# Two attention and feed-forward layers: the row maxima's products over all 72 rows on the whole TensorE array, and one load for each head's stack

## The chip, the core and the metric

One core of one Trainium2 chip runs the kernel as one program. The metric is the time of one execution on the device in microseconds (us). TensorE does the matrix products and writes to PSUM, VectorE and ScalarE compute and read PSUM out, GpSimd computes in SBUF, and SyncE issues most of the DMAs.

## What is computed

Two transformer layers over x of 8 x 512 x 128, each with a normalisation, attention of 16 heads of 8 dimensions and a feed-forward part (a block-quantised one in the first layer, 9 experts in the second). The change touches attention, which both layers have alike:

```python
xn = _layernorm(x, axis=-1)
# for each of 8 sequences of 512 tokens, 16 heads, d = 8
scores = jnp.einsum('bthd,bshd->bhts', q, k) / np.sqrt(HEAD_DIM)
weights = jax.nn.softmax(scores, axis=-1)
attn = jnp.einsum('bhts,bshd->bthd', weights, v).reshape(B, T, C)
x = x + attn @ w_out + b_out + ffn(xn)
```

## The kernel before, in words

**Precision by parts.** q and k are split into three bf16 parts each (`parts`, NP = 3). A score is the sum over the nine pairs of parts and over the 8 dimensions of a head, so it is one matmul over 9 x 8 = 72 rows, a "stack". Before the exponential the row's maximum must be taken off. It is computed first, from products alone, negated, split into two bf16 rows (`nm_hl`) and put under the stack of q as two more rows, against ones in the stack of k. So the scores of layer l come from `ks[l]` and `qs[l]` over 74 rows.

**Two passes over the scores.** The first pass is `maxima` (a pair of heads hp, a tile t of 128 tokens: two products of 128 x 512 into the two banks of a pair buffer `mx`; VectorE reduces both at once, L743) and `tile_maxima` (one product into a bank of the ring, one head and tile at a time, reduced at L747). It uses `products` (L1039): only 8 of the 9 pairs of parts, NQK = 8, which are HALF = 64 rows. Heads with even number keep these in partitions 0 to 63, odd ones in 64 to 127 (`main_rows`), so the two products of a pair lie in different halves of the array. The second pass is `scores` (L1091), on the whole array: 74 rows for even heads, all 128 for odd ones, whose unused rows hold zeros. Its results are exponentiated by ScalarE (L563) and weighted sums follow (`weighted_sums`, L1083).

**The order of TensorE** is written out by hand in `turn`, one turn for each of the 8 sequences (seven in a loop, then "last"). A turn has: the slots 3 to 15 of layer 0's scores and sums; the projections, with four pairs of the next sequence's layer 0 maxima; the nine experts, four chunks each, where a chunk is one product `expert_hidden` (L970), then zero or two pairs of maxima (`maxima_of_chunk`), then a quarter of the output of the expert before (`expert_out`, L1141, 8 matmul records); and the 16 slots of layer 1's scores and sums, of which slots 1 to 12 also hold two `tile_maxima` of layer 0. In a full turn 24 of the chunks have two pairs (experts 0 to 8: 1, 2, 2, 2, 4, 4, 3, 3, 3); in the last one only the 16 of layer 1 (experts 3 to 7). VectorE follows the same list and has between the reductions, once for each expert, `add_expert` (L831). There are two pair buffers and two ring banks.

**Stacks.** SyncE stores the parts to DRAM (`store_parts`, eight DMAs: six for the 8 pairs in `scratch`, two for the ninth in `rest`), waits for them, and loads them back (`load_stacks`): for each head one DMA of 64 rows for k and one for q, and behind eight or sixteen heads four DMAs with the ninth pair's 8 rows (`rest_rows`). The maxima wait for the 64 rows (`stack_in`), the scores for the rest too (`rest_in`). `max_rows_of` puts the maxima's two rows in, four DMAs, since even and odd heads have them in different partitions. `set_ones` on GpSimd fills zeros and ones once, four memsets a layer.

**Ahead of the loop** the first sequence's layer 0 goes through the same steps up to slot 2 of its scores, with all 32 pairs of its maxima.

Of the kernel before, what the change touches and what calls it, by code (L numbers as in the profile page):

```python
# [12 lines left out]
P = 128  # L13
# [3 lines left out]
NP = 3  # L17
NQK = NP * NP - 1
HALF = NQK * HD
# [31 lines left out]


def main_rows(u):

    return slice(u * HALF, u * HALF + HALF)


def rest_rows(u):

    return slice(HALF - HD, HALF) if u else slice(HALF, HALF + HD)  # L60


def max_row(u, a):

    return HALF - HD - 2 + a if u else HALF + HD + a


def score_rows(u):

    return slice(0, P) if u else slice(0, HALF + HD + 2)  # L70

# [102 lines left out]
def two_layers(nc, x, w_qkv, w_out0, b_out0, w_gate, w_up, w_down, wqT, wkT, wvT, woT, bq, bk, bv, bo,  # L174
               wr1, br1, wr2, br2, w1, b1, w2, b2, scratch, rest, out):
    ring, accs, mxs = ring_uses()
    ctx = ExitStack()
    with ctx:
# [83 lines left out]
        rest_in = [sem("rest_in0"), sem("rest_in1")]  # L262
# [9 lines left out]
        N_WEIGHT_DMAS, N_FP4_DMAS, N_STORES, N_STACK, N_ROWS = 17, 7, 16 * 8, 16 * 4, 16 * 4  # L272
# [42 lines left out]
        def _(sp):  # L315
# [40 lines left out]
            def store_parts(l, values):  # L356
# [4 lines left out]
                by_row = scratch[l].rearrange("m h (d n) t -> m (h d) n t", n=NQK)  # L361
                last_row = rest[l].rearrange("m h d t -> m (h d) t")
                for i in range(NP):
                    n = slice(NP * i, min(NP * i + NP, NQK))
                    width = n.stop - n.start
                    sp.dma_start(by_row[0, :, n, :], parts[:, i:i + 1, 0, :].broadcast_to([P, width, T])).then_inc(scratch_out, 16)
                    sp.dma_start(by_row[1, :, n, :], parts[:, 0:width, 1, :]).then_inc(scratch_out, 16)
                for m in range(2):
                    sp.dma_start(last_row[m], parts[:, NP - 1, m, :]).then_inc(scratch_out, 16)
                sp.wait_ge(scratch_out, stored)  # L370

            def load_stacks(l, first, last):

                for h in range(first, last):
                    for m, dst in ((1, ks[l]), (0, qs[l])):
                        sp.dma_start(dst[main_rows(h % 2), h, :], scratch[l, m, h]).then_inc(stack_in[l][h // 2], 16)
                for m, dst in ((1, ks[l]), (0, qs[l])):
                    for u in range(2):
                        heads = slice(first + u, last, 2)
                        sp.dma_start(dst[rest_rows(u), heads, :], rest[l, m, heads].rearrange("h d t -> d h t")).then_inc(rest_in[l], 16)  # L380
# [929 lines left out]
```

## Time and profile before

| | us |
|---|---|
| median of 3 runs | 1623.88 |
| lowest, highest | 1618.66, 1624.66 |
| the profiled execution, own time | 1616.24 |
| its span, first to last instruction | 1614.5 |

| engine | busy us | share | instructions |
|---|---|---|---|
| TensorE, matmul (PE) | 1465.2 | 91% | 8221 |
| TensorE, weight load (PEld) | 663.5 | 41% | 8253 |
| VectorE (DVE) | 1112.0 | 69% | 2019 |
| ScalarE (ACT) | 822.1 | 51% | 1007 |
| GpSimd (POOL) | 102.7 | 6% | 138 |

The mean granted clock of TensorE is 0.966 of its 2.4 GHz. Matmul records overlap, since they are pipelined: the time that a product takes of the engine is read from the start of one to the start of the next, not from a record's length. An fp32 product of 512 columns appears as two records. In the views, PEld is the load of a matmul's stationary operand.

### The profile page before, as it was taken

To read this page: it belongs to the slowest core of one execution; us is meant where nothing else is said; L and a number is where in the kernel's file an instruction comes from. 1 tells how busy PE (TensorE), PEld (TensorE's weight loads), DVE (VectorE), ACT (ScalarE), POOL (GpSimd) and SP (SyncE) were. 2 spreads that over 40 slices of the span, in tenths; PEclk is the share of its full clock that TensorE was granted. 3 is DMA by queue.
4 is the path that set the end of the run, shared out by engine and by line. 5 is a ranking of instruction groups with operands and counts; after the bars stand their busy time and mean duration, and the time that the engine had idled before them with its cause. 6 is when DMAs were issued, how large, how long until landed. Compare 5 with 4: busy or idle time off the path is not lost.

```text
span 1614.5 us, 23856 instructions
## 1 busy us (share of the span) xinstructions
PE 1465.2 (91%) x8221; PEld 663.5 (41%) x8253; DVE 1112.0 (69%) x2019; ACT 822.1 (51%) x1007; POOL 102.7 (6%) x138
## 2 busy tenths in 40 slices
PE   2689999999989999889998999999998999997997
PEld 1124552245523554245532455234542355423561
DVE  8976884778756787567956688477875678653660
ACT  1164238742576426754277423874257642684336
POOL 5001000110000100010001100001000100001000
PEclk7689999999999999999999999999999999997999
DMA  4404300241002400034000420024100240000300
GB/s 114 160 16 140 87 2 9 68 129 47 2 16 87 128 22 2 16 113 123 2 2 30 148 73 1 9 72 130 42 2 16 91 130 16 2 9 28 90 2 7
DMA packets 93994, 87.90 MB, mean 54 GB/s; under 512 B 12890, under 2 KB 93091, under 8 KB 93619
## 3 DMA queue, kind: packets, MB, share of 16 engines
q1 hardware_dynamic: 92258, 83.59, 17.1%
q0 software_dynamic: 672, 2.16, 0.5%
q8 instruction: 77, 1.26, 0.3%
q10 hardware_dynamic: 944, 0.54, 0.1%
q14 instruction: 43, 0.34, 0.1%
HBM read 45.87 MB, written 39.85 MB: 53 GB/s over the span
## 4 chain that ended last, share of the span: by engine, by line
PE 53%; DVE 21%; issue 14%; DVEq 5%; ACT 4%; POOL 2%; SPq 0%; DMA 0%; ACTq 0%; POOLq 0%
PE ring L970 15%; PE sums L1141 14%; DVE nm L743 8%; PE mx L1091 8%; PE sums L1083 7%; PE mx L1039 5%; ACT ex L563 3%; DVEq L825 2%; PE ring L976 2%; DVE macc L831 2%; PE ring L1039 2%; DVE xn L671 1%; PE ring L965 1%; POOL parts L470 1%; DVE h_sb L719 1%
## 5 line engine op out<-in xcount | busy, mean ns | idle before, releaser
L563 ACT ACTIVATE ex<-mx 128x1024 f32<-128x1024 f32 x512 | 497.2, 1027 | 162.2 <-PE mx L1091 161.7
L743 DVE TENSOR_REDUCE nm<-mx 128x2 f32<-128x1024 f32 x428 | 501.2, 1216 | 85.6 <-PE mx L1039 81.4
L605 ACT ACTIVATE ex<-ring,b_sb 128x512 f32<-128x512 f32 x288 | 197.1, 687 | 421.5 <-PE ring L970 421.4
L1141 PEld LDWEIGHTS sums<-w_sb,ex 128*128 128x128 f32 x2304 | 283.5, 191 | 94.8 <-issue 89.9
L1141 PE MATMUL sums<-w_sb,ex 128*128 128x128 f32 x2304 | 319.3, 283 | 0.4
L970 PE MATMUL ring<-xnT,w_sb 128*128 128x512 f32 x576 | 297.6, 602 | 2.0 <-ACT ex L605 2.0
L1091 PE MATMUL mx<-qs,ks 74*128 74x512 bf16 (+1 forms) x992 | 274.8, 385 | 15.7 <-ACT ex L563 6.6
L1083 PE MATMUL sums<-ex,vs 128*18 128x512 f32 x2048 | 269.0, 600 | 14.4 <-issue 13.8
L1091 PEld LDWEIGHTS mx<-qs,ks 128*128 128x128 bf16 (+1 forms) x1024 | 75.9, 98 | 261.8 <-ACT ex L563 235.4
L1039 PE MATMUL mx<-ks,qs 64*128 64x512 bf16 x856 | 149.4, 396 | 36.0 <-DVE nm L743 34.8
L747 DVE TENSOR_REDUCE nm<-ring 128x1 f32<-128x512 f32 x168 | 108.2, 686 | 72.3 <-PE ring L1039 71.9
L1039 PEld LDWEIGHTS mx<-ks,qs 64*128 64x128 bf16 x856 | 34.3, 94 | 220.2 <-issue 112.0
L831 DVE SCALAR_TENSOR_TENSOR macc<-sums,w,macc 128x128 f32<-128x128 f32 x288 | 81.1, 344 | 40.7 <-PE sums L1141 30.6
L970 PEld LDWEIGHTS ring<-xnT,w_sb 128*128 128x128 f32 x576 | 88.5, 192 | 23.7 <-ACT ex L605 8.8
L1083 PEld LDWEIGHTS sums<-ex,vs 128*18 128x18 f32 x2048 | 35.4, 96 | 107.5 <-issue 105.0
L766 DVE COPY work<-sums 128x512 f32<-128x512 f32 x32 | 22.0, 687 | 81.1 <-PE sums L1083 81.1
L475 POOL DMA_DIRECT2D out<-macc x8 | 6.4, 799 | 1012.1 <-DVE macc L783 1012.1
L470 POOL TENSOR_TENSOR parts<-qk_f,parts 128x512 bf16<-128x512 f32 x32 | 36.4, 1158 | 222.7 <-DVE parts L683 222.7
L736 DVE TENSOR_TENSOR acc<-acc,ring 128x512 f32<-128x512 f32 x8 | 5.5, 688 | 51.1 <-PE ring L1018 51.1
L965 PE MATMUL ring<-ident,xn 128*128 128x128 f32 x64 | 11.4, 304 | 28.4 <-DVE xn L671 28.4
L516 ACT COPY hqT<-ring 128x512 f32<-128x512 f32 (+1 forms) x40 | 22.7, 593 | 22.0 <-PE ring L965 22.0
L1039 PE MATMUL ring<-ks,qs 64*128 64x512 bf16 x168 | 32.8, 387 | 0.0
(135 smaller groups left out, 1017.2 us busy)
## 6 DMA issues: line engine op xcount, KB each, us to landing
scratch<-parts SPq DMA_DIRECT2D x64, 384.0 KB, 4.0
ks<-scratch SPq DMA_DIRECT2D x256, 64.0 KB, 2.2
qs<-scratch SPq DMA_DIRECT2D x256, 64.0 KB, 2.2
scratch<-parts SPq DMA_DIRECT2D x32, 256.0 KB, 4.1
w_sb<-w SPq DMA_DIRECT2D x2, 2304.0 KB
rest<-parts SPq DMA_DIRECT2D x32, 128.0 KB, 3.2
x_sb<-x SPq DMA_DIRECT2D x8, 256.0 KB, 2.8
out<-macc POOLq DMA_DIRECT2D x8, 256.0 KB, 3.8
```

What stands on the lines that cost most here:

```text
L470: last = pool.tensor_tensor(parts[:, 2, m, :], qk_f[:, m, :], parts[:, 1, m, :], ALU.subtract)
L563: act.activation(ex[:, ex_buffer(l, k), 2 * i:2 * i + 2, :], mx[bank][:, :, :], ACT.Exp, scale=SCALE).then_inc(mx_free[bank], 1)
L605: act.activation(ex[:, e % 2, c, :], bank[:, :], ACT.Silu, bias=b1_sb[:, e * EC + c:e * EC + c + 1]).then_inc(free, 1)
L743: dve.tensor_reduce(nm[l][:, t, h:h + 2], mx[bank][:, :, :], AX.X, ALU.max, negate=True).then_inc(mx_free[bank], 1)
L747: dve.tensor_reduce(nm[0][:, t, h:h + 1], bank[:, :], AX.X, ALU.max, negate=True).then_inc(free, 1)
L825: dve.drain()
L831: last = dve.scalar_tensor_tensor(macc[:, t, :], acc[bank][:, t * P:(t + 1) * P], w9[:, t, e:e + 1], macc[:, t, :], ALU.mult, ALU.add)
L970: pe.matmul(bank[0:rows, 0:width], lhsT, rhs, start=True, stop=True).then_inc(full, 1)
L1039: return pe.matmul(bank, qs[l][r, h, t * P:(t + 1) * P], ks[l][r, h, :], start=True, stop=True)
L1083: last = pe.matmul(acc[bank][32 * j:32 * j + 2 * VW, :], values[:, start:start + 2 * VW], ex[:, ex_buffer(l, k), j, :], start=q == 0 and s ...
L1091: return pe.matmul(bank, ks[l][r, h, s * P:(s + 1) * P], qs[l][r, h, :], start=True, stop=True)
L1141: last = pe.matmul(acc[bank][:, t * P:(t + 1) * P], ex[:, e % 2, c, t * P:(t + 1) * P], w2_sb[:, e, c, :], start=c == 0, stop=c == EC - 1)
```

## The change

The stack of each head has all 72 rows in partitions 0 to 71 (`SK`), and the maxima's rows are 72 and 73 for every head (`SKM` = 74). `products` runs over the 72 rows, all nine pairs of parts, and `scores` over 74 for every head. The array `rest`, its stores, loads and waits are gone: six stores, one load for each head and operand, two DMAs for the rows of maxima. The ones are set by one memset of partitions 64 to 127 of `ks` for each layer, and `qs` isn't set.

```diff
-NQK = NP * NP - 1
-HALF = NQK * HD
+SK = NP * NP * HD
+SKM = SK + 2
...
-        N_WEIGHT_DMAS, N_FP4_DMAS, N_STORES, N_STACK, N_ROWS = 17, 7, 16 * 8, 16 * 4, 16 * 4
+        N_WEIGHT_DMAS, N_FP4_DMAS, N_STORES, N_STACK, N_ROWS = 17, 7, 16 * 2 * NP, 16 * 4, 16 * 2
...
-                for m in range(2):
-                    sp.dma_start(last_row[m], parts[:, NP - 1, m, :]).then_inc(scratch_out, 16)
...
                 for h in range(first, last):
                     for m, dst in ((1, ks[l]), (0, qs[l])):
-                        sp.dma_start(dst[main_rows(h % 2), h, :], scratch[l, m, h]).then_inc(stack_in[l][h // 2], 16)
-                for m, dst in ((1, ks[l]), (0, qs[l])):
-                    for u in range(2):
-                        heads = slice(first + u, last, 2)
-                        sp.dma_start(dst[rest_rows(u), heads, :], rest[l, m, heads].rearrange("h d t -> d h t")).then_inc(rest_in[l], 16)
+                        sp.dma_start(dst[0:SK, h, :], scratch[l, m, h]).then_inc(stack_in[l][h // 2], 16)
...
                 for a in range(2):
-                    for u in range(2):
-                        r = max_row(u, a)
-                        sp.dma_start(qs[l][r:r + 1, first + u:last:2, :], nm_hl[u:last - first:2, a, :]).then_inc(done, 16)
+                    sp.dma_start(qs[l][SK + a:SK + a + 1, first:last, :], nm_hl[0:last - first, a, :]).then_inc(done, 16)
...
-            set_ones(0)
+            pool.memset(ks[0][64:P, :, :].bitcast(FP32), TWO_ONES).then_inc(ones_set, 1)
...
             def products(l, bank, h, t):
 
-                r = main_rows(h % 2)
-                return pe.matmul(bank, qs[l][r, h, t * P:(t + 1) * P], ks[l][r, h, :], start=True, stop=True)
+                return pe.matmul(bank, qs[l][0:SK, h, t * P:(t + 1) * P], ks[l][0:SK, h, :], start=True, stop=True)
...
-                r = score_rows(h % 2)
-                return pe.matmul(bank, ks[l][r, h, s * P:(s + 1) * P], qs[l][r, h, :], start=True, stop=True)
+                return pe.matmul(bank, ks[l][0:SKM, h, s * P:(s + 1) * P], qs[l][0:SKM, h, :], start=True, stop=True)
...
-                pe.wait_ge(rest_in[1], (it + 1) * N_STACK)
                 pe.wait_ge(nm_row_in[1], it * N_ROWS + N_ROWS)
```

## Rows read from the trace of the kernel before

**Rows 1.** The page's part 4: the chain that ended last, by engine, by line.
```profile
PE 53%; DVE 21%; issue 14%; DVEq 5%; ACT 4%; POOL 2%; SPq 0%; DMA 0%; ACTq 0%; POOLq 0%
PE ring L970 15%; PE sums L1141 14%; DVE nm L743 8%; PE mx L1091 8%; PE sums L1083 7%; PE mx L1039 5%; ACT ex L563 3%; DVEq L825 2%; PE ring L976 2%; DVE macc L831 2%; PE ring L1039 2%; DVE xn L671 1%; PE ring L965 1%; POOL parts L470 1%; DVE h_sb L719 1%
```

**Rows 2.** The page's part 5: groups, xcount | busy, mean ns | idle before.
```profile
L743 DVE TENSOR_REDUCE nm<-mx 128x2 f32<-128x1024 f32 x428 | 501.2, 1216 | 85.6 <-PE mx L1039 81.4
L1039 PE MATMUL mx<-ks,qs 64*128 64x512 bf16 x856 | 149.4, 396 | 36.0 <-DVE nm L743 34.8
```

**Rows 3.** Timeline of PE, experts 6 and 5: start us, us, what, idle before.
```profile
589.72 1.02 PE L970 MATMUL ring<-xnT,w_sb 128*128 128x512 f32 x2
590.58 1.05 PE L1141 MATMUL sums<-w_sb,ex 128*128 128x128 f32 x8
591.47 1.02 PE L970 MATMUL ring<-xnT,w_sb 128*128 128x512 f32 x2
592.43 0.60 PE L1039 MATMUL mx<-ks,qs 64*128 64x512 bf16 x4
592.96 1.16 PE L1141 MATMUL sums<-w_sb,ex 128*128 128x128 f32 x8
593.96 1.02 PE L970 MATMUL ring<-xnT,w_sb 128*128 128x512 f32 x2
```

**Rows 4.** Timeline of PE: maxima that wait for VectorE, in experts 5, 6, 8.
```profile
583.29 0.39 PE L1039 MATMUL mx<-ks,qs 64*128 64x512 bf16 x2 [0.74 <-DVE nm L743]
...
594.91 0.75 PE L1039 MATMUL mx<-ks,qs 64*128 64x512 bf16 x4
...
614.64 0.39 PE L1039 MATMUL mx<-ks,qs 64*128 64x512 bf16 x2 [0.19 <-DVE nm L743]
```

**Rows 5.** Timelines of PE and PEld: scores between expert outputs, and both kinds' weight loads.
```profile
620.23 1.03 PE L1091 MATMUL mx<-qs,ks 74*128 74x512 bf16 x4
621.09 1.95 PE L1141 MATMUL sums<-w_sb,ex 128*128 128x128 f32 x16
...
592.42 0.11 PEld L1039 LDWEIGHTS mx<-ks,qs 64*128 64x128 bf16 x4 [0.76 <-issue]
...
620.12 0.64 PEld L1091 LDWEIGHTS mx<-qs,ks 74*128 74x128 bf16 x4
```

**Rows 6.** Timeline of DVE, from the addition in expert 5 to the next.
```profile
579.85 1.13 DVE L831 SCALAR_TENSOR_TENSOR macc<-sums,w,macc 128x128 f32<-128x128 f32 x4 [0.17 <-issue]
580.89 4.61 DVE L743 TENSOR_REDUCE nm<-mx 128x2 f32<-128x1024 f32 x4
...
591.00 1.12 DVE L831 SCALAR_TENSOR_TENSOR macc<-sums,w,macc 128x128 f32<-128x128 f32 x4 [0.17 <-issue]
```

**Rows 7.** Timelines of PE and ACT: one slot of layer 1 with two tiles.
```profile
625.14 1.04 PE L1091 MATMUL mx<-qs,ks 74*128 74x512 bf16 x4
626.12 0.39 PE L1039 MATMUL ring<-ks,qs 64*128 64x512 bf16 x2
626.43 1.05 PE L1083 MATMUL sums<-ex,vs 128*18 128x512 f32 x8
...
625.79 1.94 ACT L563 ACTIVATE ex<-mx 128x1024 f32<-128x1024 f32 x2 [0.34 <-PE mx L1091]
```

**Rows 8.** Timeline of POOL and DVE ahead of the loop.
```profile
9.55 5.58 POOL L481 MEMSET ks<- 32x2048 f32 x3
...
30.10 1.22 DVE L702 TENSOR_SCALAR qsc<-amax 128x22 f32<-128x22 f32 x1
...
31.76 0.18 DVE L707 TENSOR_SCALAR qrs<-qrs 128x22 f32<-128x22 f32 x1
...
50.98 13.66 DVE L743 TENSOR_REDUCE nm<-mx 128x2 f32<-128x1024 f32 x12
```

**Rows 9.** Timelines of SP and PE: a stack load's issue, and the first product on it.
```profile
514.70 0.60 SPq L376 DMA_DIRECT2D qs<-scratch  x1
...
518.84 0.39 PE L1039 MATMUL mx<-ks,qs 64*128 64x512 bf16 x2
```

**Rows 10.** Windows: the stretch, busy us by engine, PEclk, DMA share, GB/s.
```profile
529.46:532.87 3.41, 3.41 (x10) 1.75 (x8) 2.37 (x3) 0.67 (x1) 0.00 (x0) 0.50 0.36 102
```

More of the change, by code:

```diff
@@ L50, in head @@
     return (g // 2 * HG + j) * 2 + g % 2
[L53 to L70, printed above, removed]
 class Ring:
@@ L174, in two_layers @@
 def two_layers(nc, x, w_qkv, w_out0, b_out0, w_gate, w_up, w_down, wqT, wkT, wvT, woT, bq, bk, bv, bo,
-               wr1, br1, wr2, br2, w1, b1, w2, b2, scratch, rest, out):
+               wr1, br1, wr2, br2, w1, b1, w2, b2, scratch, out):
     ring, accs, mxs = ring_uses()
@@ L418, in turn @@
                     load_max_rows(0, rows0)
-            sp.wait_ge(ones_set, 4)
+            sp.wait_ge(ones_set, 1)
             store_parts(0, stack_values(0, 0))
@@ L475, in store_out @@
                 pool.dma_start(out_rows[bass.ds(it * T, T), :].rearrange("(t p) c -> p t c", p=P), macc[:, :, :]).then_inc(macc_free, 16)
-            def set_ones(l):
-                for n, (rows, first, value) in enumerate([(qs[l][0:HALF], 1, 0.0), (ks[l][0:32], 1, 0.0),
-                                                          (ks[l][32:HALF], 1, TWO_ONES), (ks[l][HALF:HALF + 32], 0, TWO_ONES)]):
-                    pool.memset(rows[:, first:NH:2, :].bitcast(FP32), value).then_inc(ones_set, 1)
-                    pool.wait_ge(ones_set, l * 4 + n + 1)
             rstd_of(0, 0)
             pool.wait_ge(rstd_ready[0], 1)
-            set_ones(0)
+            pool.memset(ks[0][64:P, :, :].bitcast(FP32), TWO_ONES).then_inc(ones_set, 1)
+            pool.wait_ge(ones_set, 1)
             third_part(0, 0)
             pool.wait_ge(p3_ready, 1)
-            set_ones(1)
+            pool.memset(ks[1][64:P, :, :].bitcast(FP32), TWO_ONES).then_inc(ones_set, 1)
+            pool.wait_ge(ones_set, 2)
             pool.wait_ge(weights_in, 16 * N_WEIGHT_DMAS)
@@ L1303 @@
     args = {name: nc.dram_tensor(name, v.shape, FP32, kind="ExternalInput").ap() for name, v in arrays.items()}
-    scratch = nc.dram_tensor("scratch", (2, 2, NH, HALF, T), BF16, kind="Internal").ap()
-    rest = nc.dram_tensor("rest", (2, 2, NH, HD, T), BF16, kind="Internal").ap()
+    scratch = nc.dram_tensor("scratch", (2, 2, NH, SK, T), BF16, kind="Internal").ap()
     out = nc.dram_tensor("out", (B, T, P), FP32, kind="ExternalOutput").ap()
-    two_layers(nc, **args, scratch=scratch, rest=rest, out=out)
+    two_layers(nc, **args, scratch=scratch, out=out)
     r = run_bass_kernel_spmd(nc, [arrays], core_ids=[0])
```

15 lines of the change are left out of this document (5 added, 10 removed).

## The prediction

> **What bounds the kernel now.** I read the chain of work that ended last first: 53% of it is TensorE (PE) and 21% VectorE (DVE), and its longest lines are the two expert products, the reductions and the maxima's own matmuls [rows 1]. So I ask of each stretch whether PE or DVE sets its pace. The groups by line give the counts: 856 products into the pair buffers, that is 428 pairs, and 428 reductions of 1.22 us [rows 2]; by the code another 7 x 12 = 84 pairs go into the ring banks. A plain chunk of the experts on PE (one hidden product, one quarter of an output) takes 0.86 + 0.89 = 1.75 us: 589.72 to 590.58 to 591.47 [rows 3]. A chunk with two pairs between them takes 0.96 + 0.53 + 1.00 = 2.49 us (591.47, 592.43, 592.96, 593.96) [rows 3]. I call these four products a quad. So a quad costs 0.73 us of PE although its own rows last 0.53: the hidden product before it and the output after it are each 0.10 longer. There PE never idles, so PE sets the pace. In experts 4 and 5, where every chunk has a quad, DVE takes its share: a quad's second pair at 583.29 has PE idle for 0.74 us until a reduction ends [rows 4], and from one addition on DVE to the next (579.85 to 591.00) it is 11.15 us, against 4 x 2.49 = 9.96 of PE alone [rows 6]. In the twelve slots of layer 1 with two tiles, PE is without a pause while ScalarE waits 0.34 us for it [rows 7].
>
> **Part 1: the products go from two halves of the array to the whole array.** Lost is their concurrency. Today two products of a quad start together, and the quad lasts 0.53; four products over 74 rows, also bf16 with 512 columns, take 621.09 - 620.23 = 0.86 us, 0.215 each [rows 5]. 72 rows are nearest to these 74, so I take 0.865 for a quad and 0.43 for a pair. Gained are the edges. The weights of half-array products are loaded only at 592.42, after 0.76 us in which nothing is loaded, while the hidden product still runs; those of the 74-row products are loaded from 620.12 on, ahead of the first matmul at 620.23 and under the product before it [rows 5]. So the 0.10 at either side should go: a chunk with a quad becomes 1.755 + 0.865 = 2.62 us instead of 2.49. A quad costs 0.135 more, where PE sets the pace.
> The Trainium skill (TensorEngine Tiling (Array Packing), Key Properties) says that changing the tiling mode drains TensorE, which agrees with those 0.10 us. The same page (Theoretical Speedup) gives half-array packing up to twice the speed for 64 rows or fewer. That rule speaks against this change; taken alone it would charge each of 512 pairs 0.215 us, some 110 us.
>
> Stage by stage, for one of the seven full turns:
> - Experts 0 to 3: 7 quads, no wait now, 7 x 0.138 = 0.97 us (2.62 against 2.482 by the starts unrounded).
> - Experts 4 and 5: I step through the two pair buffers. Reductions follow each other every 1.13 us (four in 4.61) and a buffer is free again 1.27 us after its reduction starts (the second of 580.89 starts at 582.02, its buffer is written at 583.29) [rows 4, 6]. A pair's reduction can start some 0.65 us after its first product (0.215 until the second starts, 0.39 of that one, 0.04 of signal; 0.39 is a row's length [rows 3]). With the expert's first quad at 0, DVE is first held by the addition and reduces from 1.57 and 2.70; the second quad comes at 2.62, waits until 2.84, its second pair until 3.97, and it ends at 4.40; the others come at 6.16 and 8.78 without a wait, the next expert's at 11.40. The same reckoning of the kernel before gives 11.25 where the trace has 11.15 [rows 6], so it is good to 0.1. Like against like, each of the two costs 11.40 - 11.25 = 0.15, together 0.30 and not 8 x 0.138 = 1.10, because part of what they took was waiting for DVE.
> - Experts 6 and 7: 3 quads each, 3 x 0.138, less the 0.14 us by which one quad of each waits for DVE (0.75 where others last 0.60 [rows 3, 4]) and which the longer quad covers: 0.27 each, 0.53.
> - Expert 8: 3 quads, less the wait at 614.64 [rows 4], 0.58 - 0.21 = 0.37 us by the starts of the pairs: 0.04.
> - Sum of the experts: 0.97 + 0.30 + 0.53 + 0.04 = 1.84 us. The last turn has only layer 1's 16 quads, those of experts 3 to 7: 0.28 + 0.30 + 0.53 = 1.11.
> - Twelve slots: from the first score (625.14) over the pair (626.12) to the sums (626.43) it is 1.29 us today, with an edge of 0.10 before the pair and one after it [rows 7]. After, six full-array products follow each other and one edge is left: 6 x 0.215 + 0.10 = 1.39, and 0.01 that the first score takes more: 1.40. So 0.107 a slot, 12 x 0.107 = 1.28 us. ScalarE's 0.34 of waiting shows that it doesn't take over.
> - Four single pairs in layer 0's projections: 0.43 against 0.32 + 0.10, about 0.1 us together.
> A full turn: 1.84 + 1.28 + 0.10 = 3.22; seven of them 22.5; with the last turn 23.7 us.
>
> **Part 2: one load of 72 rows for a head, no loads of a rest.** Sixteen stack loads of 72 rows take the place of those of 64, at 0.60 us of issue each [rows 9], and the four rest loads behind them go, with two of eight stores. No transfer gets nearer to the end: in layer 0 the first head pair's fourth load is issued at 514.70, and the first product on it runs at 518.84 [rows 9]. Even if 72 rows took half as long again as 64, that is 0.3 us of issue for each of four loads, 1.2 us, and the load issued at 514.70 would be late by no more than the stores that went give back. Bounds: -0.5 to +0.5 us a turn; I take 0. What hides it is those 4 us between issue and use; without them a late load would cost its lateness once a turn. The PE waits for the rest are removed; none of them is what PE idles for, so 0. The loads of the rows of maxima fall from four to two at a time, which matters only ahead of the loop, below.
>
> **Part 3: the constants, ahead of the loop.** Three of the four memsets on GpSimd last 5.58 us together, and a second set follows; the new ones cover half the elements in one piece, an estimated 3.6 us instead of 7.4 each. DVE's small tensor-scalar operations are held by them: one of 22 elements at 30.10 takes 1.22 us, where its like at 31.76 takes 0.18 [rows 8]. That one is freed (-1.0), others are held as long by one long memset as by two short ones (-0.3 to +0.4). Two row loads less ahead of the first x load, at 0.60 an issue [rows 9]: up to -1.2, I take -0.9. Against it: in the first maxima DVE sets the pace (12 reductions in 13.66 us [rows 8]). Should PE have half its clock there, as in [rows 10], a pair takes 2 x 0.43 = 0.86 instead of 0.43, and a reduction is ready some 0.09 us late on every second pair: for 24 pairs 24 x 0.045 = +1.1. Together -1.1, bounds -3 to +2.
>
> **Sum.** 23.7 - 1.1 = 22.6 us on the profiled execution, 1616.24 us (span 1614.5): 1639. That execution was quicker than all three runs, 1618.66 to 1624.66. On their median, 1623.88, it is 1646.
>
> **Rivals.**
> A, the edges stay: 72-row products lie between fp32 products and pay 0.10 at each side as now. For: the slots' scores keep such an edge toward the sums [rows 7]. Against: the 74-row products between expert outputs have none [rows 5]. A quad then costs 0.33 more; with the waits that it covers 5.8 us a turn of experts, 12 x 0.215 in slots, 4 x 0.215 in projections: 9.2 x 7 + 3.5 = 68, less 1.1: 67, 1691 on the median.
> B, not slower: PE's clock. In every turn PE idles before the second norm's transposes, and then 529.46 to 532.87 runs at 0.50 of 2.4 GHz with PE busy for all 3.41 us [rows 10]; six turns show this one drop, and near the start of the loop and in the last turn there are three more, with two of them longer. One short drop costs half its length, 1.7 us; all together some 18 us. The new turn is 3.2 us longer, so the idle stretch falls elsewhere in the clock's own rhythm. If all drops vanished: 1616.2 + 22.6 - 18 = 1621, 0.3% above, on the median 1629. It decides once at least 15 of the 18 us come back. Against: the idle stretch itself stays as long as it is.
> C, the same clock the other way: the loop's first 2 us of idle start to cause a drop as well, 8 x 1.7 = +14: 1661.
> D, the stacks are late: one load's lateness a turn; at 1 us, +7: 1654.
>
> **How the numbers follow.** The forecast (PE pays 0.11 to 0.14 a quad or slot, drops about as now) has 0.72; A 0.06; B 0.10; C 0.07; D 0.05. The likeliest gives 1646. B's 1629 and C's 1661 with a little for the runs' spread make the range 1628 to 1664, which leaves out A and part of the rest. A measurement of this kernel can tell about 0.5%, 8 us, from no change. B gives the 0.08 of no change and, if the start gives back more too, 0.02 of faster; everything else is slower, 0.90.
>
> **What would show it.** Right: the maxima's matmuls at 72 rows start 0.215 apart, their weights load while the product before runs, a chunk with a quad lasts 2.62 us, the slots' period grows from 2.28 to 2.39, experts 4 and 5 take 11.3 to 11.5 us, and PE's idle for reductions shrinks. Wrong: a chunk with a quad at 2.8 (A), a table of the granted clock with fewer or more stretches at 0.50 (B, C), PE waiting for a stack load (D), or DVE running ahead of PE in experts 4 and 5, which would show that I sized their waits badly.

## The result, and the profile after

| | before | after |
|---|---|---|
| median of 4 runs each, us | 1621.99 | 1639.3 |
| lowest, highest | 1618.66, 1624.66 | 1638.69, 1639.9 |
| the profiled execution, own time | 1616.24 | 1639.9 |
| its span | 1614.5 | 1637.6 |
| its mean granted clock | 0.966 | 0.967 |

The ratio is 1.0109, with a 95% interval of 1.0085 to 1.0132: the change makes the kernel 1.1% slower. Between the medians lie 17.3 us, between the two profiled executions 23.1 us of span. That difference has a cause of its own, and the experiments come back to it.

The chain that ended last, the page's part 4 of the kernel after, by engine and by line (before: [rows 1]):

```profile
PE 59%; DVE 18%; issue 14%; ACT 4%; DVEq 3%; POOL 2%; DMA 0%; SPq 0%; ACTq 0%; POOLq 0%
PE ring L934 16%; PE sums L1103 14%; PE mx L1002 9%; PE mx L1053 8%; PE sums L1046 7%; DVE nm L707 6%; ACT ex L527 3%; PE ring L1002 2%; PE ring L940 2%; PE ring L929 1%; DVE xn L635 1%; DVEq L789 1%; POOL parts L439 1%; DVE h_sb L683 1%; DVE h_sb L673 1%
```

The lines have moved up by 36 to 38: the maxima's products are L1002 now, the hidden product L934, the expert output L1103, the reductions L707 and L711, the scores L1053. TensorE's share of the chain went from 53 to 59%, that of the maxima's products in it from 5 to 9%, and VectorE's fell from 21 to 18%. The groups say the same (busy us, mean ns, then the idle time before them and what ended it; before: [rows 2]):

```profile
L707 DVE TENSOR_REDUCE nm<-mx 128x2 f32<-128x1024 f32 x428 | 502.9, 1218 | 99.6 <-PE mx L1002 99.4
L1002 PE MATMUL mx<-ks,qs 72*128 72x512 bf16 x856 | 239.3, 394 | 22.6 <-DVE nm L707 21.0
```

A reduction costs what it cost (1218 against 1216 ns). TensorE is busy with the products for 239.3 us instead of 149.4, waits for reductions 21.0 us instead of 34.8, and VectorE waits for the products 99.4 us instead of 81.4.

The timeline of TensorE in the experts (start us, us, what, idle before), with one chunk without maxima and one with four of them, as in [rows 3], and two rows of its weight loads:

```profile
598.31 1.02 PE L934 MATMUL ring<-xnT,w_sb 128*128 128x512 f32 x2
599.17 1.05 PE L1103 MATMUL sums<-w_sb,ex 128*128 128x128 f32 x8
600.06 1.02 PE L934 MATMUL ring<-xnT,w_sb 128*128 128x512 f32 x2
600.92 1.03 PE L1002 MATMUL mx<-ks,qs 72*128 72x512 bf16 x4
601.78 1.06 PE L1103 MATMUL sums<-w_sb,ex 128*128 128x128 f32 x8
602.68 1.02 PE L934 MATMUL ring<-xnT,w_sb 128*128 128x512 f32 x2
...
600.49 0.10 PEld L1002 LDWEIGHTS mx<-ks,qs 72*128 72x128 bf16 x1 [0.24 <-issue]
600.92 0.53 PEld L1002 LDWEIGHTS mx<-ks,qs 72*128 72x128 bf16 x3 [0.33 <-issue]
```

The plain chunk takes 0.86 + 0.89 = 1.75 us, as before. The one with a quad takes 0.86 + 0.86 + 0.90 = 2.62 (600.06 to 602.68). The hidden product before a quad lasts 0.86 again and not 0.96, the output behind it 0.90 and not 1.00, and the first weights are loaded at 600.49, under the hidden product, where they used to load only as the product started [rows 5]. This is the chunk that the prediction laid out, to 0.01 us.

**Where the 23.1 us lie.** I cut both traces at the same instructions (first products of each expert, of each layer's sums) and took differences, after minus before:

| stretch | us |
|---|---|
| ahead of the loop | +1.1 |
| experts 1 to 8, seven full turns | 7 x 1.80 = +12.6 |
| experts of the last turn | +1.2 |
| slots of layer 1, seven turns | 7 x 1.11 = +7.8 |
| projections and expert 0's begin, eight turns | -8.6 |
| loop's first slots, eight turns | +6.9 |
| from a turn's last sums to the next turn, and the end | +2.1 |
| sum | +23.1 |

Of the last +2.1, 1.2 lie at the end, where TensorE's last products ran at half clock, and 0.9 in the pauses between turns. In the row of the projections stands the one quad of expert 0 too. The two large rows besides the experts and slots are not the work of the maxima: they are stretches of half clock that left one place and came up in another, as these windows of the kernel after show (stretch, then us, busy us by engine, PEclk, DMA share, GB/s; before: [rows 10]):

```profile
482.20:485.60 3.40, 3.23 (x16) 0.53 (x16) 2.78 (x14) 0.00 (x0) 1.03 (x1) 0.50 0.24 69
536.80:540.20 3.40, 3.40 (x9) 1.64 (x8) 2.47 (x3) 0.69 (x1) 0.00 (x0) 0.51 0.00 0
871.40:874.80 3.40, 3.40 (x17) 0.53 (x10) 2.87 (x15) 0.00 (x0) 1.03 (x1) 0.51 0.15 43
```

The second is the old place, in the projections ahead of the experts; one of the full turns still has it. The first and third are new: right after the pause in which TensorE waits at the loop's start. Before, six turns had a drop in the projections and none of these six had one at the loop's start; after, one has it in the projections and four at the loop's start. A drop that goes from the projections gives back 1.4 to 1.5 us, one at the loop's start takes 1.61 to 1.66.

### The profile page after: what moved, and what is told of

Read it like the earlier page. It is cut to its first block, busy times and chain, and to the rows that moved or that the text cites. A ratio compares the mean times of both kernels' runs of the same rounds, so it can differ in the third digit from the quotient of the medians.

```text
span 1637.6 us, 23699 instructions
## 1 busy us (share of the span) xinstructions
PE 1509.7 (92%) x8253; PEld 724.2 (44%) x8253; DVE 1110.4 (68%) x2019; ACT 822.0 (50%) x1007; POOL 95.0 (6%) x132
## 4 chain that ended last, share of the span: by engine, by line
PE 59%; DVE 18%; issue 14%; ACT 4%; DVEq 3%; POOL 2%; DMA 0%; SPq 0%; ACTq 0%; POOLq 0%
PE ring L934 16%; PE sums L1103 14%; PE mx L1002 9%; PE mx L1053 8%; PE sums L1046 7%; DVE nm L707 6%; ACT ex L527 3%; PE ring L1002 2%; PE ring L940 2%; PE ring L929 1%; DVE xn L635 1%; DVEq L789 1%; POOL parts L439 1%; DVE h_sb L683 1%; DVE h_sb L673 1%
## 5 line engine op out<-in xcount | busy, mean ns | idle before, releaser
L707 DVE TENSOR_REDUCE nm<-mx 128x2 f32<-128x1024 f32 x428 | 502.9, 1218 | 99.6 <-PE mx L1002 99.4
L1103 PEld LDWEIGHTS sums<-w_sb,ex 128*128 128x128 f32 x2304 | 298.3, 191 | 62.8 <-issue 34.2
L1103 PE MATMUL sums<-w_sb,ex 128*128 128x128 f32 x2304 | 301.2, 275 | 0.2
L934 PE MATMUL ring<-xnT,w_sb 128*128 128x512 f32 x576 | 296.9, 602 | 2.0 <-ACT ex L569 2.0
L1053 PE MATMUL mx<-qs,ks 74*128 74x512 bf16 x1024 | 282.6, 385 | 11.4 <-ACT ex L527 6.5
L1046 PE MATMUL sums<-ex,vs 128*18 128x512 f32 x2048 | 276.3, 615 | 15.3 <-issue 14.7
L1002 PE MATMUL mx<-ks,qs 72*128 72x512 bf16 x856 | 239.3, 394 | 22.6 <-DVE nm L707 21.0
L1053 PEld LDWEIGHTS mx<-qs,ks 74*128 74x128 bf16 x1024 | 76.5, 98 | 265.8 <-ACT ex L527 216.5
L1002 PEld LDWEIGHTS mx<-ks,qs 72*128 72x128 bf16 x856 | 73.6, 99 | 214.4 <-issue 107.0
L711 DVE TENSOR_REDUCE nm<-ring 128x1 f32<-128x512 f32 x168 | 108.3, 686 | 80.1 <-PE ring L1002 80.1
L934 PEld LDWEIGHTS ring<-xnT,w_sb 128*128 128x128 f32 x576 | 88.7, 192 | 22.1 <-ACT ex L569 8.4
L1002 PE MATMUL ring<-ks,qs 72*128 72x512 bf16 x168 | 50.1, 379 | 0.0
```

The source lines that it names most:

```text
L707: dve.tensor_reduce(nm[l][:, t, h:h + 2], mx[bank][:, :, :], AX.X, ALU.max, negate=True).then_inc(mx_free[bank], 1)
L711: dve.tensor_reduce(nm[0][:, t, h:h + 1], bank[:, :], AX.X, ALU.max, negate=True).then_inc(free, 1)
L934: pe.matmul(bank[0:rows, 0:width], lhsT, rhs, start=True, stop=True).then_inc(full, 1)
L1002: return pe.matmul(bank, qs[l][0:SK, h, t * P:(t + 1) * P], ks[l][0:SK, h, :], start=True, stop=True)
L1046: last = pe.matmul(acc[bank][32 * j:32 * j + 2 * VW, :], values[:, start:start + 2 * VW], ex[:, ex_buffer(l, k), j, :], start=q == 0 and s ...
L1053: return pe.matmul(bank, ks[l][0:SKM, h, s * P:(s + 1) * P], qs[l][0:SKM, h, :], start=True, stop=True)
```

## The experiments

Each ran beside the kernel before on the same chip; ratios are to that. "The stretch of expert 4" is from the first output product of one expert to that of the next, the first of the two with four quads.

### One half of the array for all

Do the edges of 0.10 us belong to products on a half of the array, or to the change between bf16 and fp32 products? The kernel after, with 64 of its 72 rows:

```diff
-                return pe.matmul(bank, qs[l][0:SK, h, t * P:(t + 1) * P], ks[l][0:SK, h, :], start=True, stop=True)
+                return pe.matmul(bank, qs[l][0:64, h, t * P:(t + 1) * P], ks[l][0:64, h, :], start=True, stop=True)
```

> The changed kernel with the maxima's products over rows 0 to 63 of every stack (left out: the ninth pair of parts and the last rows of the eight), so all products lie in one half of the array, one behind the other. My theory (what the change pays is lost concurrency, what it gets back is the 0.10 us edge on either side of half-array products): products 0.215 us apart as in the changed kernel, but with both edges back, so a chunk with a quad lasts 2.8 us instead of 2.62, a slot's pair 0.53 with its edge before it; the time is about 1680 us, 40 to 45 above the changed kernel, ratio to the kernel before 1.03 to 1.04. Rival (the edges belong to two halves being at work together, not to 64 rows): the same as the changed kernel, 1639, ratio 1.01. Rival (cost goes with rows): a little under 1639.

Measured: 1704.4 us (1699.38 to 1708.13), ratio 1.0498 (1.046 to 1.0535), slower than the kernel after by 65 us although it multiplies fewer rows. TensorE's timeline:

```profile
598.75 1.02 PE L934 MATMUL ring<-xnT,w_sb 128*128 128x512 f32 x2
599.71 1.03 PE L1002 MATMUL mx<-ks,qs 64*128 64x512 bf16 x4
600.67 1.16 PE L1103 MATMUL sums<-w_sb,ex 128*128 128x128 f32 x8
601.66 1.02 PE L934 MATMUL ring<-xnT,w_sb 128*128 128x512 f32 x2
...
602.62 0.60 PE L1002 MATMUL mx<-ks,qs 64*128 64x512 bf16 x2
...
602.62 0.11 PEld L1002 LDWEIGHTS mx<-ks,qs 64*128 64x128 bf16 x2 [0.76 <-DVE nm L707]
```

The hidden product takes 0.96 again (598.75 to 599.71), the output 0.99, and the weights load only at 602.62, together with the product's start and after 0.76 us of nothing, as in [rows 5]. So the edges belong to products on 64 rows, and the change from 64 to 72 rows is what removes them; the types are the same in both. A third part of the price I had not reckoned with: the quad lasts 0.96 and not 0.86. Its products still start 0.215 us apart; the 0.10 more lies behind the last of them, before the output starts. Two views cut close show it, of this run and of the kernel before:

```profile
600.15 0.59 PE L1002 MATMUL mx<-ks,qs 64*128 64x512 bf16 x2
600.67 0.38 PE L1103 MATMUL sums<-w_sb,ex 128*128 128x128 f32 x1
```

```profile
592.43 0.60 PE L1039 MATMUL mx<-ks,qs 64*128 64x512 bf16 x4
592.96 0.49 PE L1141 MATMUL sums<-w_sb,ex 128*128 128x128 f32 x2
```

Here two products from 600.15 take 0.52 until the output, not 0.43. In the kernel before, four side by side are two steps of 0.215, again 0.43, and take 0.53. So the third 0.10 was there before the change too, hidden in the quad's 0.53. A chunk costs 2.91 us against 2.62. Over a turn the experts take 5.4 us more and the slots 1.2, some 50 us of the 65 in all; the rest lies ahead of the loop, in the projections and in stretches of half clock (mean clock 0.961). My expectation of the size was too small, since I had given this third border nothing.

### Two halves on the new layout

Is anything of the rest of the change (stores, loads, memsets, rows of maxima) worth time? The kernel after, with the products side by side on two halves again. The odd heads' operand on rows 64 to 127 is a stand-in with the same shape:

```diff
-                return pe.matmul(bank, qs[l][0:SK, h, t * P:(t + 1) * P], ks[l][0:SK, h, :], start=True, stop=True)
+                r = slice(64 * (h % 2), 64 * (h % 2) + 64)
+                left = ks if h % 2 else qs
+                return pe.matmul(bank, left[l][r, h, t * P:(t + 1) * P], ks[l][r, h, :], start=True, stop=True)
```

> The changed kernel with its one-load stacks, its memsets and its two row loads kept, but a pair's two products side by side again: even heads over rows 0 to 63, odd heads over rows 64 to 127, where the data are a stand-in (left out: the odd heads' true maxima; softmax doesn't change with what is taken off). It isolates the loads, stores and memsets. My theory (they are off the path): the time of the kernel before less up to 2 us, ratio 0.998 to 1.001, chunks with a quad at 2.48 and experts 4 at 11.16 us. Rival (part of the 17 us comes from stack loads of 72 rows or from their stores): the ratio stays at 1.003 or more, with waits on DMA in the trace.

Measured: 1622.22 us (ten runs, 1616.27 to 1631.1), ratio 1.0014 (0.9988 to 1.004): no change that can be measured. At equal granted clock (the lines are drawn further below) its runs stand 0.5 us under those of the kernel before. Cut as above, all experts and slots stand within 0.01 us of the kernel before; only ahead of the loop, at the drops and in the pause between turns is there a difference. So the loads, the stores, the memsets and the 74-row scores cost and bring nothing that can be told, and all that the change costs comes with one line, the products over 72 rows.

### Half the reduction, after and before

The prediction lets the waits for VectorE hide part of a quad's price. Take VectorE out of the way in both kernels: the reductions read 256 of the 512 columns.

```diff
-                dve.tensor_reduce(nm[l][:, t, h:h + 2], mx[bank][:, :, :], AX.X, ALU.max, negate=True).then_inc(mx_free[bank], 1)
+                dve.tensor_reduce(nm[l][:, t, h:h + 2], mx[bank][:, :, 0:256], AX.X, ALU.max, negate=True).then_inc(mx_free[bank], 1)
...
-                dve.tensor_reduce(nm[0][:, t, h:h + 1], bank[:, :], AX.X, ALU.max, negate=True).then_inc(free, 1)
+                dve.tensor_reduce(nm[0][:, t, h:h + 1], bank[:, 0:256], AX.X, ALU.max, negate=True).then_inc(free, 1)
```

> The changed kernel with every reduction of maxima over the first 256 of 512 columns (left out: the other columns), so VectorE never sets the pace in the experts. To be read against e4. My theory (in experts 4 and 5 VectorE hides part of the price): a chunk with a quad lasts 2.62 everywhere, four of them 10.5 us instead of 11.42, total about 1610 to 1620. Rival (VectorE hides nothing): experts 4 and 5 stay near 11.4 and the distance to e4 equals that of the two kernels, 17 to 23 us.

> The kernel before with every reduction of maxima over the first 256 of 512 columns (left out: the other columns). My theory: a chunk with a quad lasts 2.48 everywhere, four of them 9.93 us instead of 11.16, total about 1575 to 1585, so that e3 is 30 to 38 us above it: 184 quads at 0.138 and 84 slots at 0.107 are 34 us with nothing hidden, against the 21 or so of the two kernels themselves. Rival: e3 minus e4 is 17 to 23 us.

Measured: after 1612.18 us (1603.92 to 1619.05, ratio 0.9933), before 1572.73 (1569.72 to 1574.57, ratio 0.97). Between the two lie 39.5 us of medians and 33.6 us of span in the profiled executions (1601.7 and 1568.1). The groups of the kernel before with half the reduction, then of the kernel after with it:

```profile
L743 DVE TENSOR_REDUCE nm<-mx 128x2 f32<-128x512 f32 x428 | 276.1, 685 | 231.9 <-PE mx L1039 231.5
L1039 PE MATMUL mx<-ks,qs 64*128 64x512 bf16 x856 | 138.7, 393 | 7.9 <-DVE nm L743 7.5
```

```profile
L707 DVE TENSOR_REDUCE nm<-mx 128x2 f32<-128x512 f32 x428 | 277.4, 686 | 258.9 <-PE mx L1002 258.0
L1002 PE MATMUL mx<-ks,qs 72*128 72x512 bf16 x856 | 232.3, 391 | 4.7 <-DVE nm L707 4.2
```

With a reduction of 685 ns TensorE waits 7.5 and 4.2 us in all, and the stretch of expert 4 is plain TensorE work: four chunks in 9.95 us (4 x 2.49) before, in 10.47 (4 x 2.62) after. The change now costs the experts 3.0 us a turn instead of 1.8. In the two experts with four quads, from one addition on VectorE to the next, it is 0.53 each (9.95 to 10.48), where with whole reductions it is 0.26 each (11.16 to 11.42). That is the price without cover. The medians are no clean measure of it: at a granted clock of 0.971, which runs of both had, the distance is 31 us and not 39.5. The other way round: cheaper reductions are worth 49 us to the kernel before and 27 to the one after by the medians (part of the 49 is clock, 0.971 against 0.963), and in experts and slots 3.8 and 2.4 us a turn. TensorE's side by side products are what lets a faster VectorE pay.

### Other places for the maxima, before and after

If VectorE sets the pace in experts 4 and 5 and TensorE in experts 1 to 3, the list of pairs can be evened. Both kernels with layer 1's pairs spread:

```diff
-M1_BY_EXPERT = [0, 0, 0, 4, 8, 8, 6, 6, 0]
+M1_BY_EXPERT = [0, 0, 0, 8, 6, 6, 6, 6, 0]
```

> The kernel before with layer 1's maxima spread as 8, 6, 6, 6, 6 pairs over experts 3 to 7 instead of 4, 8, 8, 6, 6; nothing left out. My theory: PE waits for reductions only behind an expert with eight pairs, some 1.3 us each time; one such expert in place of two saves 1.2 us in each of eight turns: 1610 to 1614, ratio 0.993 to 0.995. Rival (the waits go with the number of pairs, wherever they are): no change, 1.000.

> The changed kernel with the same spread, 8, 6, 6, 6, 6. My theory: four chunks with quads in a row cost it 11.42 us instead of 10.48, a wait of 0.94; one of two such waits goes in each turn, 0.9 x 8 = 7 us: 1632, ratio 1.006 to 1.008. Rival: no change against the changed kernel, 1.011.

and the kernel before with both lists changed, once flat and once with more of layer 0 in expert 0:

```diff
-M0_BY_EXPERT = [2, 4, 4, 0, 0, 0, 0, 0, 6]
-M1_BY_EXPERT = [0, 0, 0, 4, 8, 8, 6, 6, 0]
+M0_BY_EXPERT = [4, 4, 0, 0, 0, 0, 0, 0, 8]
+M1_BY_EXPERT = [0, 0, 2, 6, 6, 6, 6, 6, 0]
```

> The kernel before with no expert of eight pairs in layer 1: layer 1's maxima 2, 6, 6, 6, 6, 6 over experts 2 to 7, layer 0's 4, 4 and 8 in experts 0, 1 and 8; nothing left out. My theory: both waits behind the eight-pair experts go (2.5 us a turn), and the quad that now stands in expert 8's first chunk, between an addition and the rows of maxima on DVE, gives back about 1: 1606 to 1612, ratio 0.990 to 0.994. Rival (expert 8 with eight pairs and the row work waits as long as experts 4 and 5 did): 1616 to 1622, 0.998 to 1.000.

```diff
-M0_BY_EXPERT = [2, 4, 4, 0, 0, 0, 0, 0, 6]
-M1_BY_EXPERT = [0, 0, 0, 4, 8, 8, 6, 6, 0]
+M0_BY_EXPERT = [6, 4, 0, 0, 0, 0, 0, 0, 6]
+M1_BY_EXPERT = [0, 0, 2, 6, 6, 6, 6, 6, 0]
```

> The kernel before with layer 1's maxima 2, 6, 6, 6, 6, 6 over experts 2 to 7 and layer 0's 6, 4 in experts 0 and 1 and 6 in expert 8; nothing left out. My theory: no expert is left in which VectorE sets the pace, so the two waits go (2.4 us a turn) and nothing comes in their place but a few tenths in expert 0, where VectorE has the router's work: 1604 to 1610, ratio 0.989 to 0.993, a little under e7. Rival: expert 0 takes as much as it gives, 1612 as e7.

| kernel | us (lowest to highest) | ratio (interval) | experts a turn | clock |
|---|---|---|---|---|
| before, even | 1613.68 (1607.24-1617.53) | 0.9949 (0.9927-0.997) | -1.5 | 0.957-0.964 |
| after, even | 1641.25 (1639.88-1648.03) | 1.0136 (1.011-1.0161) | -1.15 | 0.955-0.959 |
| before, flat | 1612.64 (1610.42-1615.38) | 0.9952 (0.9933-0.9971) | -1.35, and +1.0 ahead of expert 1 | 0.964-0.968 |
| before, flatter | 1613.57 (1612.07-1614.28) | 0.9949 (0.993-0.9968) | -3.6, and +3.3 ahead of expert 1 | 0.965-0.968 |

(What stands ahead of expert 1 is taken between turns that both have a drop of the clock there.) The experts got shorter in all four. In both even kernels it was a little more than reckoned (1.2 and 0.9 a turn). In the flat one it was much less than the 3.5 reckoned: 3.6 us went in the stretches of experts 2 to 5, and 2.25 came back in those of experts 7 and 8, since expert 8 now has eight pairs: the rival that its expectation names. The whole followed only in part. In the kernel after, evened, I had looked for 1632 us and found no gain: the loop's begin lost what the experts won. Windows of that kernel (columns as above), with two stretches of half clock that the kernel after hasn't:

```profile
867.00:884.00 17.00, 16.62 (x60) 3.54 (x60) 14.15 (x44) 5.99 (x7) 1.03 (x1) 0.51 0.06 17
1068.00:1082.00 14.00, 14.00 (x52) 3.02 (x44) 11.97 (x35) 6.03 (x7) 1.03 (x1) 0.52 0.00 1
```

At each TensorE works nearly without a pause for 14 to 17 us at 1.2 GHz; in the trace they cost 5.7 and 4.5 us against the same stretch of the kernel after, where each had a drop of 3.4 us already. In the flatter one, expert 0 has three quads with no output product between them, and VectorE is at the router's work as they begin: TensorE waits 0.56, 0.74 and 0.50 us for reductions there, and with the two more quads' own time 3.3 of the 3.6 us are given back before expert 1. These three variants of the kernel before are the quickest here that compute the whole: 8 to 9 us below it, so below both kernels of the study, and alike within their intervals. But they got there in two ways. At equal granted clock (by the lines below) the even one is 12.4 us under the kernel before, the flat one 3.0, the flatter one 1.5, and the kernel after evened 10.0 under the kernel after. So evening the pairs took away the waits in both kernels, and its clock, 0.960 and 0.959 in the median, hid part or all of it; the flat and the flatter one won mostly by a better clock, 0.966 and 0.967.

### The kernel after once more

The first four runs of the kernel after lay within 1.2 us, those of the kernel before within 6. Is it steadier, or was that a draw?

> The changed kernel once more beside the others, with more executions. Theory (its four times agree because it has fewer stretches at half clock than the kernel before, not by luck): mean granted clock 0.967 to 0.969 in all, 1638 to 1640, while the kernel before spreads over 0.960 to 0.965 and 1616 to 1626. Rival (a draw for each execution): a spread of 8 us or more here too, and a ratio up to 1.015.

Measured: 1639.44 us, six runs from 1636.46 to 1651.66, ratio 1.0127 (1.0096 to 1.0159). It was a draw. The runs also say what varies. Each has its mean granted clock, and within a kernel the time follows it:

| granted clock (some of the rows) | kernel before, of 49 runs beside the experiments, us | kernel after, of 10 runs, us |
|---|---|---|
| 0.956 | 1632.8 | |
| 0.959 to 0.960 | 1624.8 to 1626.1 (7 runs) | 1651.7 |
| 0.963 | 1619.0 to 1622.1 (14) | |
| 0.965 | 1616.4 to 1618.6 (7) | 1643.9 |
| 0.967 to 0.968 | 1612.8 | 1639.2 to 1639.9 (3) |
| 0.969 to 0.970 | | 1636.5 to 1638.7 (4) |

A straight line through each kernel's runs misses by 0.8 to 0.9 us; it falls by 1.6 us for each 0.001 of clock before, and by 1.4 after. At 0.965 the lines stand at 1617.6 and 1643.0: at equal clock the change costs 25.4 us. That is good to some 2 us and not better: the mean clock is a share of a span that is itself 1.5% longer after (at equal microseconds of half clock it is 24.8), and a stretch of half clock costs more or less by what TensorE does in it. Its runs had the better clock on the whole (0.967 in the median of ten, 0.963 before), and that gave some 6 us back, so that the medians lie only about 18 us apart. It stays open whether the better clock comes from the change or from where the turns happened to fall: its turn is 3 us longer, and the evened version of the same kernel had 0.955 to 0.959.

### Filling the pause

Could work in TensorE's pauses keep the clock up? Two more fp32 products of constants, results unused, run ahead of TensorE's wait for the second norm, in the flatter kernel and in the kernel after:

```diff
+                bank, full = to_ring(part, it, "xT1")
+                for n in range(2):
+                    pe.matmul(bank[:, :], ident[:, :], w1_sb[:, 0, :], start=True, stop=True)
```

> e9 with two fp32 products of constants, 1.7 us, put into the idle time of PE ahead of the second norm's transposes; their results are overwritten, nothing left out. My theory on the clock (the stretches at 0.50 in the projections follow that idle time): they vanish there, each of them 1.4 us, so up to 7 x 1.4 = 10 us where an execution had them all and on average some 5: ratio about 0.003 below e9, mean clock up by 0.003. Rival (the drops come from elsewhere, or the fill delays the transposes): no change or 1 us a turn more.

> The changed kernel with the same fill. Theory: drops in the projections vanish, those at the loop's start stay: 1632 to 1637, ratio 1.007 to 1.010 against the 1.0109 and 1.0127 of the changed kernel. Rival: as the changed kernel, 1636 to 1652.

Measured: 1626.99 us (twelve runs, 1618.76 to 1629.74; ratio 1.0029, interval 1.001 to 1.0048) where the flatter kernel without them has 1613.57, and 1649.91 (1645.78 to 1663.95; 1.0201, 1.0162 to 1.024) where the kernel after has 1639.4. The drops in the projections of the full turns are indeed gone: from the last product of layer 0's sums to the first output product it is 29.74 us in each of them, while in the flatter kernel it is 31.00 where a drop falls in it. But something else grew, the pause at the loop's start. TensorE's timelines there, of the flatter kernel, then of the filled one:

```profile
475.16 3.34 PE L1083 MATMUL sums<-ex,vs 128*18 128x512 f32 x16 [2.34 <-issue]
```

```profile
478.15 3.62 PE L1083 MATMUL sums<-ex,vs 128*18 128x512 f32 x16 [3.97 <-issue]
```

2.34 us of waiting for nothing that the profile shows became 3.97; all six passages from one turn of the loop to the next grew, by 0.9 to 1.7 us, and longer stretches of half clock followed. With the kernel after it is +1.1 to +1.6 in four of six, and -0.2 and +0.2 in the others. Where the pause belongs the traces show. The loop has seven turns, so its end jumps back six times; the first turn is entered, and the "last" turn reached, without a jump back. Two passages of the kernel before, one inside the loop and the one out of it into the last turn:

```profile
473.61 0.60 PE L1091 MATMUL mx<-qs,ks 74*128 74x512 bf16 x2
476.60 1.91 PE L1083 MATMUL sums<-ex,vs 128*18 128x512 f32 x16 [2.40 <-issue]
...
1429.80 0.60 PE L1091 MATMUL mx<-qs,ks 74*128 74x512 bf16 x2
1430.32 1.91 PE L1083 MATMUL sums<-ex,vs 128*18 128x512 f32 x16
```

The same products follow each other, and the second time nothing lies between them. It is so in all thirteen traces, the filled ones too: 2.1 to 4.0 us at each of the six jumps back, none at the other two passages. So the pause is the jump's. Why two more products in the loop's body lengthen it, no run here tells; that stays open. As a way to hold the clock the edit is a loss.

## Why the prediction was right, and where it was not

The forecast was 1646 us, within 1628 to 1664, and slower; 1639.3 were measured, slower by 17.3 us.

**The edges go, and the quad takes 0.865: right.** A chunk with a quad is 2.62 us, as said. Rival A (edges stay, 1691) falls with the trace, and the run on one half of the array shows why: edges come and go with 64 rows against 72. The Trainium skill (TensorEngine Tiling (Array Packing), Key Properties) says that a change of the tiling mode drains TensorE; the rows agree, at 0.10 us a side. The same page's Theoretical Speedup, "Up to 2×", taken alone an estimate of 110 us, would have been far off: the change at equal clock costs some 25.

**The experts: right, 1.80 us a turn against 1.84, and 1.16 against 1.11 in the last.** Experts 1 to 8 one by one: 0.26, 0.24, 0.36, 0.26, 0.03, 0.26, 0.26, 0.13. (The stretches start at output products, so a quad of one expert may count in the stretch before.) The stepped account of experts 4 and 5 gave 11.40 us from one addition to the next. The timeline of VectorE, to be laid beside [rows 6]:

```profile
588.28 1.13 DVE L795 SCALAR_TENSOR_TENSOR macc<-sums,w,macc 128x128 f32<-128x128 f32 x4 [0.17 <-issue]
589.33 4.61 DVE L707 TENSOR_REDUCE nm<-mx 128x2 f32<-128x1024 f32 x4
594.56 2.36 DVE L707 TENSOR_REDUCE nm<-mx 128x2 f32<-128x1024 f32 x2 [0.62 <-PE mx L1002]
597.18 2.36 DVE L707 TENSOR_REDUCE nm<-mx 128x2 f32<-128x1024 f32 x2 [0.26 <-PE mx L1002]
599.70 0.61 DVE L795 SCALAR_TENSOR_TENSOR macc<-sums,w,macc 128x128 f32<-128x128 f32 x2 [0.17 <-issue]
```

It is 599.70 - 588.28 = 11.42. The kernel before has 11.15 between the same two additions [rows 6], so each of the two experts costs 0.27 and not 0.15: the stepping was right for the new kernel, but its error of 0.10 for the old one (11.25) wasn't made again, and so didn't cancel. The expert behind them gives it back, 0.12 from addition to addition (9.50 to 9.62) where I had 0.27. The sum of 1.80 came out right with that luck in it. In the timeline two of VectorE's waits for TensorE (0.62 and 0.26) show that TensorE sets the pace for the third and fourth quad, while the second still waits for VectorE. TensorE's timeline has that wait, and it is 0.53 where it was 0.74 [rows 4]:

```profile
591.73 0.60 PE L1002 MATMUL mx<-ks,qs 72*128 72x512 bf16 x2 [0.53 <-DVE nm L707]
```

That waits cover part of the price was an argument in the prediction. The pair of kernels with half the reduction shows it: almost without the waits the experts pay 3.0 us.

**The slots: the mechanism right, the sum 0.17 us a turn too large.** A slot is 1.40 us from score to sums and 2.39 in all, as forecast (TensorE, kernel after):

```profile
634.49 1.04 PE L1053 MATMUL mx<-qs,ks 74*128 74x512 bf16 x4
635.36 0.60 PE L1002 MATMUL ring<-ks,qs 72*128 72x512 bf16 x2
635.89 1.05 PE L1046 MATMUL sums<-ex,vs 128*18 128x512 f32 x8
636.88 1.04 PE L1053 MATMUL mx<-qs,ks 74*128 74x512 bf16 x4
```

635.89 - 634.49 = 1.40, 636.88 - 634.49 = 2.39. Twelve of them are 1.28 us, but layer 1 took only 1.11 longer. Behind the slots TensorE transposes the maxima and waits for the last reduction; that wait shrank. The kernel after, then the kernel before:

```profile
660.99 0.60 PE L929 MATMUL ring<-ident,nm 128*16 128x128 f32 x4 [0.18 <-DVE nm L711]
```

```profile
650.65 0.60 PE L965 MATMUL ring<-ident,nm 128*16 128x128 f32 x4 [0.39 <-DVE nm L747]
```

In the two kernels with half the reduction layer 1 costs the full price, 1.33 a turn. The step that failed is small and general: I had asked in the experts which wait a longer TensorE covers, and not at the end of the slots.

**The loads cost nothing: right.** The run with two halves shows it for all of part 2. Their issue got quicker, which my bounds had not looked for. Two rows of the queue of loads on SyncE, kernel after, to be laid beside [rows 9]:

```profile
33.29 0.36 SPq L351 DMA_DIRECT2D ks<-scratch  x1
33.69 0.37 SPq L351 DMA_DIRECT2D qs<-scratch  x1
```

A load of 72 rows is issued in 0.37 us, one of 64 rows took 0.60. I had allowed for half as long again. No wait of TensorE ends with a DMA in either trace, so rival D falls, and the quicker issue brings nothing either.

**Ahead of the loop: wrong, +1.1 where I had -1.1.** The sum itself was off: -1.0, -0.9 and +1.1 make -0.8, and -1.1 only with the lowest value of the memset's other holds. The run with two halves tells the layout from the products. It reaches the first weighted sum at 90.42, the kernel before at 90.72, the kernel after at 91.83. So the products cost 1.4 where I had 1.1, and the rest gave 0.3 where I had 1.9.

The reductions under half clock were right: 14 of them take 16.66 us instead of 15.91, the 12 of [rows 8] 14.07 instead of 13.66, together 1.16 against 1.1. The first x load is issued 0.4 us earlier (90.09 instead of 90.48), not 0.9, and nothing of this stage waits for it. VectorE's operations beside the memset, in the kernel after (with GpSimd's memset) and in the kernel before:

```profile
23.43 3.51 POOL L452 MEMSET ks<- 64x4096 f32 x1
...
24.11 3.04 DVE L677 TENSOR_SCALAR binade<-work 128x384 int32<-128x384 int32 x1
...
30.20 0.18 DVE L666 TENSOR_SCALAR qsc<-amax 128x22 f32<-128x22 f32 x1
31.68 0.34 DVE L677 TENSOR_SCALAR binade<-work 128x352 int32<-128x352 int32 x1
```

```profile
24.40 1.33 DVE L713 TENSOR_SCALAR binade<-work 128x384 int32<-128x384 int32 x1
25.81 1.88 DVE L715 TENSOR_SCALAR binade<-binade 128x384 f32<-128x384 f32 x1
```

The small operation at 30.20 is free indeed, 0.18 us instead of the 1.22 of [rows 8]. The one long memset (3.5 us, as estimated) holds L677 for 3.04 us, where its like takes 0.34: it ends 0.21 us behind the memset (27.15 against 26.94). The two short memsets before held two operations, for 1.33 and 1.88 us. One long hold cost 0.2 us more than two short ones, within my bounds. The Trainium skill (SBUF — State Buffer, Who interferes with whom) says that GpSimd and VectorE share a port pair, and that whoever has it keeps it for the whole instruction; these rows agree.

So VectorE gained what I had said. The step that failed is the next one: I took its gain for a gain of the stage. With two halves the first reduction of maxima comes 0.95 us earlier than before (41.77 against 42.72), and after five of them 0.3 is left (50.69 against 50.98), since VectorE has to wait (0.77 us at 44.90) for TensorE's feed-forward products, which run at half clock until 45.3. In the kernel after, the first quad, at half clock, took 1.71 us instead of 0.97; its first reduction was 0.6 us earlier (42.09) and after five 0.2 was left (50.75).

**The clock: rivals B and C both came about, in part.** I had B take all drops away, or C add some at the loop's start, each for all turns at once. What happened is both: five of six drops in the projections went, some 1.45 us each, and in the last turn a stretch of half clock was 6.8 us long instead of 13.7, 1.3 us; together 8.6 us; and four at the loop's start came, 1.65 each, 6.6 us. With 1.2 us that the end lost to half clock (from 1629.1 on, before only from 1611.5 of 1614.5), these nearly cancel. (B's 18 us for all nine drops are less than half their length, 22 of 44 us; the short ones gave back 1.4 to 1.5 each and not 1.7.) The forecast's "drops about as now" held for the sum of these two executions, and by luck; over the ten runs the clock gave back some 6 us; where a drop falls in a turn I could not foretell then and can't now.

**Adding to the median: the base 2 us too high, and a better clock.** The sum of 22.6 us was made against the profiled execution (1616.24), and there it gives 1639, where 1639.9 was found. I then took it to the median of three runs, 1623.88, and said 1646, 6.7 too much. With 49 more runs of the kernel before, its median is 1621.2 to 1621.6 on three chips: the three runs had come out on its upper side, by some 2.5 us. The rest is clock: the changed kernel's runs had the better one, and their median lies 18 us above that of the kernel before and not 22.6.

Like for like the change costs more than forecast. The rows of the stretches with the clock's own share left out give 24 us: the 22.6 and 2.2 ahead of the loop and 0.9 between the turns, less 1.5 that I had too much for slots and experts. (The 0.9 may be chance: the six pauses sum to 13.5 to 14.9 us over the eleven traces without a fill.) The lines at equal clock give 25.4. The last microsecond has no place; it is less than such a comparison can tell.

## What to carry to other kernels

Count what an engine pays from the start of one product to the start of the next, and at both borders of a group: here four products two by two on the halves of the array save 0.43 us a quad against one behind the other, and the borders take 0.30 of it back, so they win by 0.13 and not by half. Ask of every longer step what wait it covers, also at the end of a stage, and try the opposite by making the other engine fast in both kernels: it shows the bare price. And where a kernel's runs spread by 1% at a fixed instruction stream, compare at equal granted clock, and stretch by stretch, before explaining a few microseconds by code: three variants with the same median here had won 12, 3 and 1.5 us.

## What the runs showed of the hardware that I had not expected

- A group of 64-row products between 128-row ones pays 0.30 us at its borders, side by side or not: the product before it 0.96 instead of 0.86 us, 0.31 instead of 0.215 behind its last product, the output 1.00 instead of 0.90. Four 64-row products one behind the other are therefore dearer than four over 72 rows, a chunk of 2.91 against 2.62 us. Only side by side did 64 rows pay here.
- The issue of a 72-row load on SyncE took 0.37 us, of a 64-row one 0.60, with the same kind of source and destination.
- The places where TensorE's clock falls to 1.2 GHz shift by edits of a few microseconds and from one execution of a kernel to the next. One drop of 3.4 us costs 1.3 to 1.7 us, and with the mean clock that they leave the kernel before goes from 1612.8 to 1632.8 us.
- At each jump back of the loop TensorE stands still for 2.1 to 2.7 us, and at no other passage between turns. Two more fp32 products in the body made it 3.7 to 4.0 at all six jumps of one kernel, for a reason that no view shows.
